# A macaron transformer layer on one core: first four rotary chunks in buffers of their own, rows sent by part, shorter plan distances at both ends, last value products ahead of the projection

## The chip, the cores and the metric

The kernel runs on one core of a Trainium2 chip. The metric is the device time of one execution in microseconds (us), lower is better. Times of the same kernel agree within about 0.3%.

## What is computed

The input x is 16 x 1024 x 256 in float32 (batch, positions, channels). The layer is a "macaron": half a feed-forward, attention, half a feed-forward, each with a layer norm in front and added to x.

```
x = x + 0.5 * ffn(layernorm(x))
x = x + attention(layernorm(x))
x = x + 0.5 * ffn(layernorm(x))

ffn(x):        prev = x shifted by one position
               xr, xk = mu_r*x + (1-mu_r)*prev,  mu_k*x + (1-mu_k)*prev
               sigmoid(xr @ W_r.T) * (relu(xk @ W_k.T)**2 @ W_v.T)
attention(x):  16 heads of size 16; q, k, v = x @ W_qkv + b_qkv
               rotary embedding on q and k; causal softmax(q k^T / 4) v
               y @ W_proj + b_proj
```

## The kernel before, in words

**Tiles.** A batch (1024 positions) is worked in 4 chunks of 256 positions (NCH). Attention takes heads in groups of 4 (G), so a batch has 4 groups and the kernel has 64, numbered n. A group's scores are worked in 12 ticks (a 512-wide query chunk by a 128-wide key block), 4 slots to a tick (one for each head): 48 slots a group (GSLOTS), 192 a batch (BSLOTS), 3072 in all. In one slot TensorE makes a score product (L585), ScalarE its exponential (L703) and, on diagonal blocks, GpSimd a causal select per tick (L922). Each tick then has value products (`pv`, L612). A softmax needs the row maximum first: 48 "units" per group, a product on TensorE (L592) and a masked maximum on VectorE (L806), run 61 slots ahead of the scores (MAX_FROM = -61). The units of one group follow those of the last without a break, so group 0 has its maxima in slots -61 to -14, group 1 from -13, group 2 from 35.

**Exact q and k in bf16.** The score products are bf16 with q and k split in three parts (high, mid, low), stacked as six 16-row terms on the partitions of `qr_sb` and `kr_sb`; a term names the part of q and of k (TERMS_Q, TERMS_K). To make them, each of the 2 x 4 rotary chunks of a batch (pair 0 or 1 of the head groups, chunk c; numbered i) runs through a chain over five engines: `r_QK` (L675, TensorE), `r_b0`, `r_b1` add the bias into `qb_sb` (L753, ScalarE), `r_swap` exchanges partitions by 4 DMAs into `sw_sb` (L525), `r_cos` (L963, GpSimd) and `r_sin` (L859, VectorE) multiply, `r_add` (L863) adds, `r_hi` (L762, ScalarE), `r_rest` (L966, GpSimd), `r_mid` (L765), `r_low` (L969) split into `part_sb`. `qb_sb` has two buffers and `sw_sb` one, so a chunk's bias waits for `r_low` of the chunk two before it, and a swap waits for `r_add` of the one before. When all 4 chunks of a pair are split, 12 DMAs of 128 KB for each group (steps `rows0` to `rows5`, one for k and one for q each, L534) carry them to `qr_sb` and `kr_sb`; the row `rows` of group n isn't planned before slot 48n - 95.

**Everything else is fitted in.** Feed-forward chunks p (`f_st`, `f_rstd`, `f_x`, `f_T`, `f_xn`, `f_dif`, `f_k`, `f_r`, then the matmul steps `f_K` L663, `f_R` L666, `f_V` L669 with `f_relu`, `f_sq`, `f_tanh`, then `f_u`, `f_xadd`), the layer norm of attention (`a_st`, `a_rstd`, `a_x`, `a_T`, `a_xn`), v (`a_V` L679, `a_vc`), the maximum's rows (`m_fin`, `m_T`, `m_copy`, `m_rows`), the output of attention (`y_copy` L787, `y_out`, `y_recip`, `y_back`, `y_in` through DRAM, `y_mul` L974), the projection (`p_P` L653 and L657, `xp` L871) and the stores are placed by `Plan`. Each step has an engine, a cost in slots' work, a start and a list of (step, number, distance): it may be placed once those steps lie at least that many slots back. The lowest start among the ready ones goes first; a matmul step also needs a free bank of two (`ps_d`). Outside slots -61 to 3071 an engine gets 2.5 times its normal work per slot. Slots are not times: each engine executes its instructions in the order of slots and waits for semaphores only. So the plan sets the order on each engine, and an empty slot costs nothing. The plan begins at slot FIRST; FIRST also sets the starts of the first batch's steps.

**Around the ends.** In the plan before, TensorE's order at the start is f_T.0, f_T.1, f_T.2, f_K.0, f_R.0, f_V.0, f_K.1, ...; the rotary chunks 0 to 3 come after one another; a_V.0 and a_V.1, then f_T.4, lie ahead of the first maximum unit and f_K.4, f_R.4, f_V.4 and r_QK.4 behind it. r_QK.7 ends in slot -1, r_low.7 is in slot 21 and the `rows` of group 2 in slots 23 to 28. At the end, p_P.60 and p_P.61 (first half of the last batch's projection) lie in slots 3073 to 3075, then the value products of the last two ticks (slot 3075), then f_T.124, f_T.125, f_K, f_R, f_V of 124 and 125, p_P.62, p_P.63, and the same for 126 and 127.

Of the kernel before, what the change touches and what calls it, by code (L numbers as in the profile page):

```python
# [18 lines left out]
CH = 256  # L19
# [10 lines left out]
NT = len(TERMS_Q)  # L30
KR = NT * HS
# [21 lines left out]
FIRST = -176  # L53


class Plan:
# [41 lines left out]
    def describe(self):  # L98
# [29 lines left out]
        for b in range(nb):  # L128
# [80 lines left out]
    def ready(self, slot, after):  # L209
        return all(k in self.slots and self.slots[k] + lag <= slot for k, lag in (((n, i), lag) for n, i, lag in after))  # L210
# [104 lines left out]
def macaron(nc, x, w_r, w_k, w_v, mu_r, mu_k, w_qk, b_qk, w_vv, b_v, w_p, b_p, rope_c, rope_s, out, nb=B):  # L315
# [6 lines left out]
    with ctx:  # L322
# [78 lines left out]
        swapped, r_cos, r_sin, r_add = sem("swapped"), sem("r_cos"), sem("r_sin"), sem("r_add")  # L401
# [81 lines left out]
        def _(eng):  # L483
# [28 lines left out]
            for slot in slots:  # L512
                for name, i in plan.at["SP"].get(slot, ()):
# [7 lines left out]
                    elif name == "r_swap":  # L521
                        sp.wait_ge(*taken_from("r_QK", i))
                        sp.wait_ge(r_add, i)
                        for q in range(4):
                            eng.dma_start(sw_sb[32 * q:32 * q + 32, :, :],  # L525
                                          qb_sb[32 * (q ^ 1):32 * (q ^ 1) + 32, i % 2, :, :]).then_inc(swapped, 16)
                    elif name[:4] == "rows":
                        b, g = divmod(i, NG)
                        ring, m, base = i % RS, g // 2, 64 * (g % 2)
                        sp.wait_ge(r_low, (2 * b + m + 1) * NCH)  # L530
                        sp.wait_ge(scored, GSLOTS * (i - RS + 1))
                        t = int(name[4:])
                        for dst, n, part in ((kr_sb, 1, TERMS_K[t]), (qr_sb, 0, TERMS_Q[t])):
# [38 lines left out]
        def _(eng):  # L572
# [110 lines left out]
            for slot in slots:  # L683
                if 0 <= slot < n_ticks * G:
# [353 lines left out]
```

## Time and profile before

| what | value |
|---|---|
| median of 3 executions | 3216.09 us (3215.34 to 3225.63) |
| profiled execution, whole | 3219.0 us |
| its span on the core | 3217.3 us |
| mean granted clock of TensorE | 0.979 |
| busy: TensorE / its weight loads | 95% / 52% |
| busy: VectorE, ScalarE, GpSimd | 77%, 68%, 46% |
| mean DMA rate | 76 GB/s |

The page cuts the span in 40 slices of 80.4 us, each digit a busy share in tenths. TensorE:

```profile
PE   5689999999999999999999999999999999999987
DVE  3678788887877878888887887888788888878852
PEclk8799999999999999999999999999999999999987
```

The reader sees 9 in all but the first three slices and the last two, and the granted clock lower only at both ends.

### The profile page before, as it was taken

What the parts mean: (1) busy time and instruction counts of PE and PEld (TensorE: products, weight loads), DVE (VectorE), ACT (ScalarE), POOL (GpSimd) and SP (SyncE); (2) the same over time, 40 slices, a digit from 0 to 9 for tenths busy, and PEclk for the clock granted to TensorE, in tenths of its full rate; (3) what the DMA queues carried; (4) which work ended last, traced back from release to release, by engine and by line L of the source; (5) the groups of instructions that cost most, each with busy time, mean ns of one, the idle gap of its engine ahead of it and who ended that gap; (6) DMA issues with size and microseconds to landing.
All of it is one profiled execution on the core that took longest, in us unless ns stands there. A gap on an engine that the chain in (4) does not pass through costs nothing.

```text
span 3217.3 us, 57438 instructions
## 1 busy us (share of the span) xinstructions
PE 3042.8 (95%) x18372; PEld 1664.5 (52%) x18372; DVE 2485.2 (77%) x8322; ACT 2182.1 (68%) x4801; POOL 1489.3 (46%) x2132
## 2 busy tenths in 40 slices
PE   5689999999999999999999999999999999999987
PEld 4434555555555555555555555555555555555434
DVE  3678788887877878888887887888788888878852
ACT  3266677777767777777776777777776777777663
POOL 4443444544544544444554444454454445444322
PEclk8799999999999999999999999999999999999987
DMA  3344244434434334433433434442443443344311
GB/s 90 50 67 79 61 84 86 76 79 74 93 59 96 77 73 88 76 87 67 96 68 75 91 72 84 80 82 69 81 97 60 85 88 75 80 74 84 74 41 34
DMA packets 201438, 245.30 MB, mean 76 GB/s; under 512 B 68269, under 2 KB 102321, under 8 KB 201137
## 3 DMA queue, kind: packets, MB, share of 16 engines
q1 hardware_dynamic: 201137, 241.63, 37.8%
q8 instruction: 147, 2.41, 0.4%
q14 instruction: 154, 1.26, 0.2%
HBM read 53.22 MB, written 51.38 MB: 33 GB/s over the span
## 4 chain that ended last, share of the span: by engine, by line
PE 81%; ACT 6%; DVE 6%; issue 3%; DMA 1%; POOL 1%; SPq 1%; POOLq 0%; DVEq 0%; ACTq 0%
PE ps_y L612 16%; PE ps_s L585 15%; PE ps_m L592 13%; PE ps_d L669 7%; PE ps_d L666 7%; PE ps_d L663 7%; PE ps_d L675 6%; PE ps_d L653 4%; ACT pt_sb L703 3%; DVE ps_m L806 3%; PE ps_d L679 3%; PE ps_d L619 3%; ACT qb_sb L753 1%; ACT xt_sb L712 1%; DVE fst_sb L819 1%
## 5 line engine op out<-in xcount | busy, mean ns | idle before, releaser
L806 DVE CUSTOM_DVE_ANT_0 ps_m<-ps_m,mask_sb 128x512 f32<-128x512 f32 (+3 forms) x3072 | 1692.4, 569 | 567.1 <-PE ps_m L592 550.8
L703 ACT ACTIVATE pt_sb<-ps_s 128x512 f32<-128x512 f32 (+3 forms) x3072 | 1470.5, 493 | 874.9 <-PE ps_s L585 852.7
L585 PE MATMUL ps_s<-qr_sb,kr_sb 99*128 99x512 bf16 (+3 forms) x3072 | 1009.4, 332 | 40.7 <-ACT pt_sb L703 30.9
L592 PE MATMUL ps_m<-kr_sb,qr_sb 96*128 96x512 bf16 (+3 forms) x3072 | 998.5, 328 | 33.6 <-DVE mx_sb L806 17.3
L922 POOL TENSOR_SCALAR_AFFINE_SELECT pt_sb<-pt_sb 128x512 f32<-128x512 f32 x512 | 334.4, 653 | 834.7 <-ACT pt_sb L703 831.7
L585 PEld LDWEIGHTS ps_s<-qr_sb,kr_sb 99*128 99x128 bf16 x3072 | 298.4, 98 | 783.6 <-ACT pt_sb L703 328.8
L612 PE MATMUL ps_y<-pt_sb,v_sb 128*32 128x512 f32 (+3 forms) x6144 | 636.8, 502 | 0.0
L806 DVE DVE_READ_ACCUMULATOR2_ANT mx_sb<- 128x1 f32 x3072 | 434.1, 141 | 0.0
L592 PEld LDWEIGHTS ps_m<-kr_sb,qr_sb 96*128 96x128 bf16 x3072 | 297.6, 97 | 168.1 <-DVE mx_sb L806 56.5
L675 PE MATMUL ps_d<-axn_sb,wqk_sb 128*128 128x256 f32 x1024 | 304.4, 396 | 3.9 <-ACT axn_sb L745 1.7
L663 PE MATMUL ps_d<-ka_sb,wk_sb 128*128 128x256 f32 x1024 | 301.9, 392 | 6.3 <-DVE ka_sb L830 4.6
L669 PE MATMUL ps_d<-wv_sb,ka_sb 128*128 128x256 f32 x1024 | 305.6, 387 | 0.0
L666 PE MATMUL ps_d<-wr_sb,dif_sb 128*128 128x256 f32 x1024 | 303.1, 384 | 1.8 <-ACT fxn_sb L727 1.8
L612 PEld LDWEIGHTS ps_y<-pt_sb,v_sb 128*32 128x32 f32 x6144 | 134.9, 109 | 259.1 <-issue 235.5
L950 POOL TENSOR_TENSOR x_sb<-x_sb,dif_sb 128x512 f32<-128x512 f32 x128 | 163.6, 1278 | 204.7 <-DVE dif_sb L842 202.9
L963 POOL TENSOR_TENSOR qb_sb<-qb_sb,cos_sb 128x512 f32<-128x512 f32 x128 | 178.0, 1390 | 118.8 <-DMA sw_sb<-qb_sb 117.4
L663 PEld LDWEIGHTS ps_d<-ka_sb,wk_sb 128*128 128x128 f32 x1024 | 194.5, 197 | 44.6 <-issue 6.4
L969 POOL TENSOR_TENSOR part_sb<-qb_sb,part_sb 128x512 bf16<-128x512 f32 x128 | 149.2, 1166 | 118.8 <-ACT part_sb L765 118.8
L675 PEld LDWEIGHTS ps_d<-axn_sb,wqk_sb 128*128 128x128 f32 x1024 | 184.1, 195 | 37.2 <-ACT fxn_sb L727 5.1
L666 PEld LDWEIGHTS ps_d<-wr_sb,dif_sb 128*128 128x128 f32 x1024 | 183.7, 193 | 31.9 <-ACT fxn_sb L727 2.6
L669 PEld LDWEIGHTS ps_d<-wv_sb,ka_sb 128*128 128x128 f32 x1024 | 180.3, 191 | 34.3
L619 PE MATMUL ps_d<-id_sb,xt_sb 128*128 128x128 f32 x768 | 125.2, 287 | 68.0 <-ACT xt_sb L712 48.7
(76 smaller groups left out, 3214.7 us busy)
## 6 DMA issues: line engine op xcount, KB each, us to landing
kr_sb<-part_sb SPq DMA_DIRECT2D x384, 128.0 KB, 4.5
qr_sb<-part_sb SPq DMA_DIRECT2D x384, 128.0 KB, 4.9
sw_sb<-qb_sb SPq DMA_DIRECT2D x512, 64.0 KB, 2.0
y_way<-yt_sb SPq DMA_DIRECT2D x128, 256.0 KB, 3.0
x_sb<-x SPq DMA_DIRECT2D x64, 256.0 KB, 2.9
yn_sb<-y_way SPq DMA_DIRECT2D x64, 256.0 KB
den_sb<-r_way SPq DMA_DIRECT2D x64, 256.0 KB
out<-x_sb SPq DMA_DIRECT2D x64, 256.0 KB, 2.2
```

The costliest lines, as they stand in the source:

```text
L585: eng.matmul(ps_s[:, slot % NS, 0:width], kr_sb[0:KR + NP, n % RS, j, kb * P:(kb + 1) * P], qr_sb[0:KR + NP, n % RS, j, q0:q0 + width], st ...
L592: eng.matmul(ps_m[:, u % NM, 0:width], qr_sb[0:KR, n % RS, j, i * P:(i + 1) * P], kr_sb[0:KR, n % RS, j, piece * QC:piece * QC + width], s ...
L612: pv_j = eng.matmul(ps_y[32 * j:32 * j + 32, QC - width:QC], v_sb[:, b % 2, kb, col:col + 32], pt_sb[:, tick % PT, j, 0:width], start=(kb ...
L619: last = eng.transpose(dst[:, cc * CH + t * P:cc * CH + (t + 1) * P], src[:, t, cc * P:(cc + 1) * P], id_sb[:, :])
L663: mm = eng.matmul(ps[:, rows], wk_sb[:, cc, cols], ka_sb[:, i % 2, cc, :], start=(cc == 0), stop=(cc == CC - 1))
L666: mm = eng.matmul(ps[:, rows], dif_sb[:, i % 2, cc, cols], wr_sb[:, cc, :], start=(cc == 0), stop=(cc == CC - 1))
L669: mm = eng.matmul(ps[:, rows], ka_sb[:, i % 2, cc, cols], wv_sb[:, cc, :], start=(cc == 0), stop=(cc == CC - 1))
L675: mm = eng.matmul(ps[:, rows], wqk_sb[:, cc, w0:w0 + P], axn_sb[:, c, cc, :], start=(cc == 0), stop=(cc == CC - 1))
L703: eng.activation(pt_sb[:, tick % PT, j, 0:width], ps_s[:, slot % NS, 0:width], ACT.Exp, scale=SCALE).then_inc(exped, 1)
L806: eng.tensor_tensor_reduce(ps_m[:, u % NM, 0:width], ps_m[:, u % NM, 0:width], mask_sb[:, m0:m0 + width], 1.0, -3e38, ALU.add, ALU.max, mx ...
L922: eng.affine_select(out=diag, in_=diag, compare_op=ALU.is_ge, fill=0.0, base=0, pattern=[[0, G], [1, P]], channel_multiplier=-1).then_inc( ...
L963: eng.tensor_tensor(qb_sb[:, i % 2, :, :], qb_sb[:, i % 2, :, :], cos, ALU.mult).then_inc(r_cos, 1)
```

## The change

It does seven things. (1) Rotary chunks 0 to 3 of the first batch keep their biased and swapped halves in `pt_sb` (the exponentials' buffer, not yet in use), each chunk in a place of its own, and don't wait for `r_low` or `r_add` of earlier chunks; chunks 4 and 5 don't wait for `r_low` either. (2) The semaphore `swapped` becomes four, one for each chunk number. (3) The six `rows` steps are sorted by part: steps 0 to 2 wait for the high parts only, 3 and 4 for the mid ones, 5 for the low ones. (4) FIRST goes from -176 to -160. (5) Distances count half (rounded up) before slot -61 and 0.4 (rounded up) from slot 3072 on. (6) Pair 1 of the first batch starts 10 slots earlier; for the last group, some distances on the way of y are shorter. (7) The value products of the last two ticks come at slot 3072, ahead of other steps, not at 3075.

```diff
-FIRST = -176
+BY_PART_Q = sorted(range(NT), key=lambda t: TERMS_Q[t])
+BY_PART_K = sorted(range(NT), key=lambda t: TERMS_K[t])
+FIRST = -160
...
-                        t = -40 + 18 * c if pair else FIRST + 32 + 6 * c
+                        t = -50 + 18 * c if pair else FIRST + 32 + 6 * c
...
-                    s("ACT", "r_b0", i, 0.36, t, ("r_QK", i, 1), ("r_low", i - 2, 1))
+                    s("ACT", "r_b0", i, 0.36, t, ("r_QK", i, 1), ("r_low", i - 2 if i >= NCH + 2 else -1, 1))
...
-                    s("SP", "r_swap", i, 3.2, t, ("r_b1", i, 1), ("r_add", i - 1, 1))
+                    s("SP", "r_swap", i, 3.2, t, ("r_b1", i, 1), ("r_add", i - 1 if i > NCH else -1, 1))
...
-                s("SP", f"rows{t}", n, 1.6, max(FIRST, at - 2 * GSLOTS + 1 + 3 * t), ("r_low", last, 2),
+                part = ("r_hi", "r_mid", "r_low")[TERMS_Q[BY_PART_Q[t]]]
+                s("SP", f"rows{t}", n, 1.6, max(FIRST, at - 2 * GSLOTS + 1 + 3 * t), (part, last, 2),
...
-                done = at + G * sum(KQ * (q + 1) for q in range(qc + 1)) + PV_AT
+                end = n == nb * NG - 1
+                done = at + G * sum(KQ * (q + 1) for q in range(qc + 1)) + (0 if end and qc == NQC - 1 else PV_AT)
...
-                s("DVE", "y_recip", k, 0.2, done + 1, ("y_out", k, 8))
+                s("DVE", "y_recip", k, 0.2, done + 1, ("y_out", k, 4 if end else 8))
...
-                    s("SP", "y_in", m, 1.6, done + 1, ("y_back", k, 6), ("y_mul", m - 1, 1), ("p_P", before, 1))
-                    s("POOL", "y_mul", m, 1.3, done + 1, ("y_in", m, 9))
+                    s("SP", "y_in", m, 1.6, done + 1, ("y_back", k, 3 if end else 6), ("y_mul", m - 1, 1), ("p_P", before, 1))
+                    s("POOL", "y_mul", m, 1.3, done + 1, ("y_in", m, 5 if end else 9))
...
+    def apart(self, slot, lag):
+
+        if slot >= self.nb * BSLOTS:
+            return math.ceil(lag * 0.4)
+        return math.ceil(lag * 0.5) if slot < MAX_FROM else lag
...
+        def swapped_of(i):
+
+            return pt_sb[:, 0, i, :].rearrange("p (k n) -> p k n", n=CH) if i < NCH else sw_sb[:, :, :]
+
+        def biased_of(i):
+
+            return pt_sb[:, 1, i, :].rearrange("p (k n) -> p k n", n=CH) if i < NCH else qb_sb[:, i % 2, :, :]
...
-                        sp.wait_ge(r_low, (2 * b + m + 1) * NCH)
+                        part, chunks = TERMS_Q[BY_PART_Q[k]], (2 * b + m + 1) * NCH
+                        if part == 0:
+                            sp.wait_ge(r_high, chunks)
+                        elif part == 1:
+                            sp.wait_ge(r_mid, chunks)
+                        else:
+                            sp.wait_ge(r_low, chunks)
...
             for slot in slots:
+                if slot == n_ticks * G:
+                    pv((n_ticks - 2, n_ticks - 1))
...
-                    act.wait_ge(r_low, i - 1)
+                    if i >= NCH + 2:
+                        act.wait_ge(r_low, i - 1)
```

## Rows read from the trace of the kernel before

**Rows 1.** The page's first part: busy time, share of the span, instructions.
```profile
PE 3042.8 (95%) x18372; PEld 1664.5 (52%) x18372; DVE 2485.2 (77%) x8322; ACT 2182.1 (68%) x4801; POOL 1489.3 (46%) x2132
```

**Rows 2.** Waits of TensorE, whole span: total us, times, longest.
```profile
PE ps_m L592 <- DMA qr_sb<-part_sb: 14.1, 2, 8.8
```

**Rows 3.** Chain that ended last, 0 to 201 us: start, us, piece.
```profile
29.57 1.73 PE ps_d L666 x8
...
53.81 2.03 DMA sw_sb<-qb_sb
...
85.29 1.16 POOL part_sb L969
86.47 0.62 SPq L534
...
93.54 9.08 DMA qr_sb<-part_sb
102.66 1.03 PE ps_m L592 x2
...
183.39 1.58 POOL part_sb L969
...
192.08 8.84 DMA qr_sb<-part_sb
```

**Rows 4.** Timeline, first feed-forward: start, us, engine, line, [idle before <- releaser].
```profile
15.37 0.88 DVE L830 SCALAR_TENSOR_TENSOR ka_sb<-dif_sb,muk_sb,fxn_sb 128x256 f32<-128x256 f32 x2 [2.51 <-POOL dif_sb L945]
...
18.67 3.62 PE L663 MATMUL ps_d<-ka_sb,wk_sb 128*128 128x256 f32 x8
...
49.01 1.89 PE L675 MATMUL ps_d<-axn_sb,wqk_sb 128*128 128x256 f32 x8
```

**Rows 5.** Timeline, rotary chunks 0 to 3 and what follows them.
```profile
51.00 0.84 ACT L753 ACTIVATE qb_sb<-ps_d,bqk_sb 128x256 f32<-128x256 f32 x2 [1.94 <-PE ps_d L675]
...
55.90 1.77 POOL L963 TENSOR_TENSOR qb_sb<-qb_sb,cos_sb 128x512 f32<-128x512 f32 x1 [2.91 <-DMA sw_sb<-qb_sb]
...
73.28 1.62 DVE L863 TENSOR_TENSOR qb_sb<-qb_sb,sw_sb 128x512 f32<-128x512 f32 x1 [1.15 <-POOL qb_sb L963]
...
83.39 1.15 POOL L966 TENSOR_TENSOR qb_sb<-qb_sb,part_sb 128x512 f32<-128x512 f32 x1 [1.29 <-ACT part_sb L762]
84.58 0.63 ACT L765 ACTIVATE part_sb<-qb_sb 128x512 bf16<-128x512 f32 x1 [1.26 <-POOL qb_sb L966]
...
92.41 0.88 DVE L830 SCALAR_TENSOR_TENSOR ka_sb<-dif_sb,muk_sb,fxn_sb 128x256 f32<-128x256 f32 x2 [8.81 <-POOL dif_sb L945]
```

**Rows 6.** Chain that ended last, from 3175 us: a feed-forward's matmul steps after idle.
```profile
3175.68 3.78 PE ps_d L663 x8
3179.47 2.22 PE ps_d L666 x8
3181.69 1.73 PE ps_d L669 x8
```

**Rows 7.** Stretches: length, busy us (instructions) PE, PEld, DVE, ACT, POOL, clock, DMA, GB/s.
```profile
100.00:110.00 10.00, 7.34 (x21) 5.22 (x22) 3.84 (x11) 1.23 (x2) 0.00 (x0) 0.58 0.29 30
...
130.00:140.00 10.00, 5.62 (x23) 3.05 (x22) 9.40 (x33) 2.43 (x5) 6.50 (x9) 0.78 0.30 44
...
150.00:160.00 10.00, 4.96 (x22) 2.43 (x21) 9.20 (x31) 1.74 (x5) 6.53 (x12) 0.81 0.01 3
...
200.00:210.00 10.00, 8.78 (x38) 2.73 (x38) 7.22 (x20) 4.06 (x11) 1.90 (x2) 0.66 0.14 30
210.00:220.00 10.00, 8.69 (x54) 4.33 (x52) 7.97 (x25) 5.69 (x14) 6.96 (x7) 0.83 0.41 69
```

**Rows 8.** Timeline of TensorE: first score, and the second wait for rows.
```profile
162.92 0.40 PE L585 MATMUL ps_s<-qr_sb,kr_sb 99*128 99x512 bf16 x1
...
200.96 0.61 PE L592 MATMUL ps_m<-kr_sb,qr_sb 96*128 96x512 bf16 x1 [5.28 <-DMA qr_sb<-part_sb]
```

**Rows 9.** Timeline, the last 60 us.
```profile
3162.58 2.05 PE L653 MATMUL ps_d<-wp_sb,yn_sb 128*128 128x256 f32 x4
...
3162.95 0.64 POOL L922 TENSOR_SCALAR_AFFINE_SELECT pt_sb<-pt_sb 128x512 f32<-128x512 f32 x1 [0.52 <-ACT pt_sb L703]
...
3168.66 0.86 PE L612 MATMUL ps_y<-pt_sb,v_sb 128*32 128x256 f32 x16
...
3199.46 3.78 PE L663 MATMUL ps_d<-ka_sb,wk_sb 128*128 128x256 f32 x8 [0.69 <-ACT fxn_sb L727]
```

**Rows 10.** Stretches as in rows 7, at the end.
```profile
3150.00:3160.00 10.00, 9.21 (x32) 1.43 (x28) 0.00 (x0) 4.74 (x11) 1.27 (x2) 0.50 0.00 0
3160.00:3170.00 10.00, 9.25 (x49) 5.40 (x48) 2.88 (x8) 1.80 (x7) 3.69 (x6) 0.67 0.00 0
```

More of the change, by code:

```diff
@@ L1 @@
+import math
 from contextlib import ExitStack
@@ L209, in ready @@
     def ready(self, slot, after):
-        return all(k in self.slots and self.slots[k] + lag <= slot for k, lag in (((n, i), lag) for n, i, lag in after))
+        return all((n, i) in self.slots and self.slots[n, i] + self.apart(slot, lag) <= slot for n, i, lag in after)
+    def apart(self, slot, lag):
+        if slot >= self.nb * BSLOTS:
+            return math.ceil(lag * 0.4)
+        return math.ceil(lag * 0.5) if slot < MAX_FROM else lag
     def place(self):
@@ L400, in macaron @@
         a_stat, a_mean, a_eps, a_pow, a_rstd, a_xt = sem("a_stat"), sem("a_mean"), sem("a_eps"), sem("a_pow"), sem("a_rstd"), sem("a_xt")
-        swapped, r_cos, r_sin, r_add = sem("swapped"), sem("r_cos"), sem("r_sin"), sem("r_add")
+        r_cos, r_sin, r_add = sem("r_cos"), sem("r_sin"), sem("r_add")
+        swapped = [sem(f"swapped{k}") for k in range(NCH)]
         r_high, r_rest, r_mid, r_low = sem("r_high"), sem("r_rest"), sem("r_mid"), sem("r_low")
@@ L522, in _ @@
                         sp.wait_ge(*taken_from("r_QK", i))
-                        sp.wait_ge(r_add, i)
+                        if i >= NCH:
+                            sp.wait_ge(r_add, i)
                         for q in range(4):
-                            eng.dma_start(sw_sb[32 * q:32 * q + 32, :, :],
-                                          qb_sb[32 * (q ^ 1):32 * (q ^ 1) + 32, i % 2, :, :]).then_inc(swapped, 16)
+                            eng.dma_start(swapped_of(i)[32 * q:32 * q + 32, :, :],
+                                          biased_of(i)[32 * (q ^ 1):32 * (q ^ 1) + 32, :, :]).then_inc(swapped[i % NCH], 16)
                     elif name[:4] == "rows":
                         b, g = divmod(i, NG)
-                        ring, m, base = i % RS, g // 2, 64 * (g % 2)
-                        sp.wait_ge(r_low, (2 * b + m + 1) * NCH)
+                        ring, m, base, k = i % RS, g // 2, 64 * (g % 2), int(name[4:])
+                        part, chunks = TERMS_Q[BY_PART_Q[k]], (2 * b + m + 1) * NCH
[5 more added lines that the diff above has]
+                            sp.wait_ge(r_low, chunks)
                         sp.wait_ge(scored, GSLOTS * (i - RS + 1))
-                        t = int(name[4:])
-                        for dst, n, part in ((kr_sb, 1, TERMS_K[t]), (qr_sb, 0, TERMS_Q[t])):
+                        for dst, n, t in ((kr_sb, 1, BY_PART_K[k]), (qr_sb, 0, BY_PART_Q[k])):
                             eng.dma_start(dst[t * HS:(t + 1) * HS, ring, :, :],
@@ L690, in _ @@
                 tick = slot // G - 1
-                if slot % G == PV_AT and 0 <= tick < n_ticks and tick % NTK not in BURST_OF:
+                if slot % G == PV_AT and 0 <= tick < n_ticks - 1 and tick % NTK not in BURST_OF:
                     pv((tick - 1, tick) if tick % NTK - 1 in BURST_OF else (tick,))
@@ L862, in dense @@
                     dve.wait_ge(r_sin, i + 1)
-                    eng.tensor_tensor(qb_sb[:, i % 2, :, :], qb_sb[:, i % 2, :, :], sw_sb[:, :, :], ALU.add).then_inc(r_add, 1)
+                    eng.tensor_tensor(biased_of(i), biased_of(i), swapped_of(i), ALU.add).then_inc(r_add, 1)
                 elif name == "b_add":
@@ L961, in dense @@
                     cos = cos_sb[:, halves(i % NCH)].rearrange("p (o n) -> p o n", o=1).broadcast_to([P, 2, CH])
-                    pool.wait_ge(swapped, 64 * (i + 1))
-                    eng.tensor_tensor(qb_sb[:, i % 2, :, :], qb_sb[:, i % 2, :, :], cos, ALU.mult).then_inc(r_cos, 1)
+                    pool.wait_ge(swapped[i % NCH], 64 * (i // NCH + 1))
+                    eng.tensor_tensor(biased_of(i), biased_of(i), cos, ALU.mult).then_inc(r_cos, 1)
                 elif name == "r_rest":
                     pool.wait_ge(r_high, i + 1)
-                    eng.tensor_tensor(qb_sb[:, i % 2, :, :], qb_sb[:, i % 2, :, :], parts_of(i, 0), ALU.subtract).then_inc(r_rest, 1)
+                    eng.tensor_tensor(biased_of(i), biased_of(i), parts_of(i, 0), ALU.subtract).then_inc(r_rest, 1)
                 elif name == "r_low":
                     pool.wait_ge(r_mid, i + 1)
-                    eng.tensor_tensor(parts_of(i, 2), qb_sb[:, i % 2, :, :], parts_of(i, 1), ALU.subtract).then_inc(r_low, 1)
+                    eng.tensor_tensor(parts_of(i, 2), biased_of(i), parts_of(i, 1), ALU.subtract).then_inc(r_low, 1)
                 elif name == "y_mul":
```

10 lines of the change are left out of this document (5 added, 5 removed).

## The prediction, made before the result was known

> **What bounds the kernel now.** I read the page first: TensorE is busy 95% of the span [rows 1], and the strip of forty slices has its gaps at both ends only. So the middle, some 3000 us, is one row of slots in TensorE's own order, and the change leaves its order nearly alone. A gain can only be the time until that row runs at its pace, and the time after it. The waits of TensorE say how much is to be had: two waits for the rows' DMAs make 14.1 us [rows 2]. The chain through the start says why: it goes from the swap DMAs to the last `r_low`, through 12 DMA issues by SP, through 9.08 us in which the last of them lands, to the first maximum at 102.66 [rows 3]. The same pattern stands once more before 200.96 [rows 3, 8]. Between them, VectorE is the fuller engine [rows 7]. The last views are those of the end [rows 6, 9, 10]: feed-forwards with a wait in front of each pair.
>
> **How I get the new order.** The plan is arithmetic with fixed costs, so I replayed its first and last hundred slots with the new distances, and then set durations from rows to the new order on each engine. That gives five terms.
>
> **Term 1, the start up to the first maximum.** *Feed-forward.* Before, f_K.0 starts at 18.67 behind f_T.2, though its input (15.37 + 0.88) is there at 16.25 [rows 4]. In the new order f_K.0 lies ahead of f_T.2 and starts at about 16.3. The halved distances also take f_V.1 behind f_T.3, a_T.0 behind f_K.2, and the first r_QK behind f_V.3 and a_T.2, where each input has been ready. Stepped on with 1.73 a matmul step [rows 3] and 0.6 for each bank that waits for ScalarE, r_QK.0 starts near 43.5 instead of 49.01 [rows 4]: 5.5 us. *Rotary.* SP issues a swap's four DMAs in 2.5 us, and the last lands 2.03 after its issue [rows 3]. With places of their own the four swaps follow one another from 46.4 on and land at 50.4, 52.9, 55.4 and 57.9. From there GpSimd is the limit. Its order is cos 0, 1, 2, rest 0, 1, cos 3, low 0, rest 2, low 1, low 2, rest 3, low 3; four times 1.77 and eight times 1.15 [rows 5] with two waits of 0.8 for swaps and one of 0.7 for r_mid give 50.5 + 18.6 = 69.1 for the end of r_low.3, before 86.45 (85.29 + 1.16) [rows 3]. r_hi.3 ends near 65.2. *Rows.* By part, the DMAs start at 65.2, not behind r_low; r_mid.3 and r_low.3 end before SP has issued the DMAs that need them. From the first issue at 86.47 to the first maximum it took 16.2 us [rows 3], and I keep all of it, since the transfers, not the issues, set it: landed at 81.4. *What is late next.* Not the rows. The new plan has f_K.4, f_R.4, f_V.4 and three quarters of r_QK.4 ahead of the first maximum, where before they lay behind it, and a_V.0 and a_V.1 now lie behind. f_K.4's input ended 93.29, 6.85 behind r_low.3 (92.41 + 0.88) [rows 5], because GpSimd's order has r_low.3 ahead of f_rstd.4. So it comes at 76.0, the step at 76.1; then 3.78 + 2.22 + 1.73 [rows 6] and 1.3 of r_QK.4 put the first maximum at 85.2. Before 102.66: **17.4 us**. The bounds: 21.3 were TensorE free when the rows land, 12 if GpSimd's waits fall 5 us worse.
>
> **A rule against this term.** VectorE's add took 1.62 us where GpSimd worked on its r_low [rows 5], though it moves no more than a swap's product with the sine; so packing both engines costs something, and I put VectorE's adds behind GpSimd's work and kept 1.77 for each cos. The Trainium skill (SBUF — State Buffer, Who interferes with whom) says that a VectorE instruction with two SBUF inputs and a GpSimd one that reads SBUF exclude each other for the whole instruction. Here the row agrees (1.62 is GpSimd's 1.15 and then some). Taken both ways, with GpSimd losing 0.5 on each of eight more instructions, the first maximum would come 4 us later.
>
> **Term 2, first maximum to first score.** 102.66 to 162.92 is 60.3 us [rows 3, 8] for 61 slots. VectorE is at 9.4 and 9.2 of 10 in two of the stretches but at 3.84 in the first, where TensorE ran f_K.4 between the maxima at a clock of 0.58 [rows 7]. With that work in front, the first maxima run at VectorE's pace. I take 5 us for this and 0.8 for f_u.4, also in front now. Against it, the m_rows of group 0 stand behind swap 7 in SP's queue (before, ahead of it): its four issues of 0.6 and a shorter distance to slot 0 cost about 1. Net **4.8 us**, between 0 and 8.
>
> **Term 3, the second wait.** r_QK.7 ends ten slots earlier, in slot -10 instead of -1, r_hi.7 comes in slot 4 and r_low.7 in slot 11, not 21, and the rows of group 2 start in slot 6 instead of 23. From r_low.7's end (184.97) to the landing it took 16 us [rows 3, 8]. Slot 35, where the first maximum of group 2 stands, was reached at 195.7. The new rows are there some 10 us ahead of it. The wait of 5.28 goes [rows 8]: **5.3 us**, certain if term 1 is right.
>
> **Term 4, after it.** After that wait the clock is 0.66 and 0.83 for 10 us each [rows 7], so 8.8 and 8.7 busy us hold at most 3.0 and 1.5 us that full clock would save, and SP, which was late with the 12 issues, is late with the rest (swaps 9 and 10, and the m_rows of group 1). I take **3 us**, between 0 and 6. The Trainium skill (TensorE: Matmul & The Clock Gate, What's actually happening) says that the throttled clock is the default and that activity releases it; the trace agrees, 0.66 stands behind the wait and 1.00 where none is.
>
> **The middle: 0.** Sorting the rows by part and four semaphores for one add no instruction. `rows` of later groups start at 48n - 95, where high and low are long done for one pair of groups; for the other, SP's rows step can come some slots earlier and wait. What is queued behind it on SP is swaps, y steps and stores, all with tens of slots in hand. No wait of TensorE for rows shows in the middle [rows 2].
>
> **Term 5, the end.** With the shorter way of y, y_mul.62 comes in slot 3059, not 3070, and p_P.60 and p_P.61 move into the last score ticks, slots 3062 to 3068. That is no gain by itself: the 8 steps are the same and run on TensorE, which is busy 9.21 of 10 us there [rows 10]. At half clock they cost as much as where they stood (four records in 2.05 [rows 9]). But the statistics of chunks 124 and 125, 3162 to 3171 before, now lie beside the ticks. The last value products then wait for GpSimd's last select (0.64, 3162.95 [rows 9]), about 1 us without cover, and end near 3170.5, 1 us later than before (3168.66 + 0.86). f_T.124 follows at once, f_K.124 at 3174.3 and not 3175.68 [rows 6]: 1.4. p_P.62 still comes behind f_V.125, by its start of 3084 against 3048, so the second wait stays, but in the new plan f_K.126 has the other bank and needn't wait the 0.69 for f_xn.127 [rows 9]: 0.6. **2 us**, between -2 and 6.
>
> **The sum.** 17.4 + 4.8 + 5.3 + 3 + 2 = 32.5 us. The profiled execution took 3219.0 (span 3217.3), which gives 3186.5 for one like it; the median of the three runs is 3216.1, 2.9 below, so I predict **3183.6**. The bounds of the terms, half used on each side, give 3172 to 3194 as this case's own range.
>
> **The rivals.**
> *Less than half reaches the end (3194 to 3204, chance 0.16).* The shorter distances put an instruction that isn't ready ahead of ones that are, in the order of GpSimd or TensorE. For it: cos 2 already stands ahead of rest 0 in my replay. Worked out: term 1 falls to 12 with the late GpSimd, term 2 to 0, term 4 to 0; with 5.3 and 0 at the end, 17 us are left, 3199.
> *The end gets its clock back (3170 to 3176, 0.14).* In the last ticks the clock is 0.50, and the projection's matmuls are where it rises (0.67) [rows 10]. If they release it inside the ticks, some 14 us of TensorE's work lie behind them up to the last value products, and up to half is saved; with 4 more of term 1, 3173. The Trainium skill (TensorE: Matmul & The Clock Gate, What's actually happening) would have it so, since activity releases the clock there.
> *It doesn't do what it says (within 0.3%, 3206 to 3226, 0.04).* The bias of chunk 2 goes without its wait, but if GpSimd's order kept chunks serial, the gain would be the 3.1 us from r_hi to r_low (83.39 to 86.45 [rows 3, 5]) twice.
> *Slower (0.04).* SP waits in order. If the rows steps that wait for high parts hold back a swap or y step by those 3.1 us for each of the 31 later pairs of groups, and that passes to TensorE, 96 us come against 32: 3280. It decides once SP's slack, tens of slots, is used up; from 1.05 us lost for each pair on, the gain of 32.5 is gone. Nothing in the waits of TensorE shows SP near that.
> The forecast's own range holds the other 0.62. The range for 8 in 10 takes in most of the clock rival and half of the first: 3171 to 3199. About 0.3% (10 us) is what a measurement of this kernel tells from no change: faster by more 0.91, within it 0.05, slower 0.04.
>
> **What would show it.** The first maximum (L592) at 85, with f_V.4 (L669) just ahead of it and no wait for `qr_sb<-part_sb` of over 1 us; the last `r_low` of chunk 3 at 69; the first score at 140; no wait near slot 35, at about 173; the last score near 3138, then one value-product group, with L653 records between the scores before it. Wrong would be a first maximum after 91 (term 1), a wait for the rows' DMAs in the second place (term 3), or a distance from the first score of group 3 to that of group 63 changed by over 3 us (the middle).

## The result and the profile after

The changed kernel takes **3179.44 us** (median of 4 runs, 3177.07 to 3184.35) against 3215.72 for the one before beside it (4 runs, 3210.74 to 3225.63): ratio 0.9885, 95% interval 0.9859 to 0.9912. The medians lie 36.3 us apart, and the interval makes that 28 to 45. Its profiled execution took 3180.46 us with a span of 3178.7, where that of before had 3219.0 and 3217.3.

The page of the changed kernel, against [rows 1] and the strips shown with the time before: TensorE has 16.7 us less of busy time for the same 18372 matmuls, so these matmuls ran at a higher clock on average; the other 21.9 of the 38.6 us between the spans are idle time gone.

```profile
PE 3026.1 (95%) x18372; PEld 1656.0 (52%) x18372; DVE 2484.0 (78%) x8322; ACT 2183.1 (69%) x4801; POOL 1489.9 (47%) x2132
...
PE   4899999999999999999999999999999999999988
...
PEclk8999999999999999999999999999999999999997
```

The waits of TensorE after the change (total us, times, longest). None for `qr_sb<-part_sb` of [rows 2] is left; the longest is now f_T.4's.

```profile
PE ps_d L645 <- ACT xt_sb L740: 54.7, 34, 19.9
...
PE ps_m L618 <- DVE mx_sb L835: 11.5, 40, 1.1
```

Its timeline through the rotary chunks (start, us, engine, line, idle before and releaser): r_QK.0 to r_QK.2 in one row, cos 0, rest 0 and rest 1 in one row, the add of chunk 2, the sine of chunk 3, the rows' first issue, r_low.3, f_T.4, f_K.4, f_V.4, the first maximum, the first score, the first maximum of group 2 (slot 35), and `y_copy.2`, where the row of slots runs at its pace.

```profile
43.73 5.45 PE L701 MATMUL ps_d<-axn_sb,wqk_sb 128*128 128x256 f32 x24 [0.62 <-DVE dif_sb L871]
...
50.69 1.77 POOL L992 TENSOR_TENSOR pt_sb<-pt_sb,cos_sb 128x512 f32<-128x512 f32 x1 [2.90 <-DMA pt_sb<-pt_sb]
...
57.48 2.71 POOL L995 TENSOR_TENSOR pt_sb<-pt_sb,part_sb 128x512 f32<-128x512 f32 x2
57.55 1.62 DVE L892 TENSOR_TENSOR pt_sb<-pt_sb 128x512 f32<-128x512 f32 x1 [1.15 <-POOL pt_sb L992]
59.10 1.64 DVE L888 TENSOR_TENSOR pt_sb<-pt_sb,sin_sb 128x512 f32<-128x512 f32 x1
...
65.73 0.61 SPq L560 DMA_DIRECT2D kr_sb<-part_sb  x1
...
68.60 1.15 POOL L998 TENSOR_TENSOR part_sb<-pt_sb,part_sb 128x512 bf16<-128x512 f32 x1 [0.74 <-ACT part_sb L794]
...
72.69 1.09 PE L645 MATMUL ps_d<-id_sb,xt_sb 128*128 128x128 f32 x4 [19.87 <-ACT xt_sb L740]
76.76 3.48 PE L689 MATMUL ps_d<-ka_sb,wk_sb 128*128 128x256 f32 x8 [2.98 <-DVE ka_sb L859]
81.80 1.89 PE L695 MATMUL ps_d<-wv_sb,ka_sb 128*128 128x256 f32 x8
84.82 0.38 PE L618 MATMUL ps_m<-kr_sb,qr_sb 96*128 96x512 bf16 x1
...
142.17 0.38 PE L611 MATMUL ps_s<-qr_sb,kr_sb 99*128 99x512 bf16 x1
...
174.75 0.38 PE L618 MATMUL ps_m<-kr_sb,qr_sb 96*128 96x512 bf16 x1
...
200.44 0.59 ACT L816 ACTIVATE yt_sb<-ps_y 128x512 f32<-128x512 f32 x1
```

The end, from the last ticks on: a projection step among the scores, the last value products, f_K.124.

```profile
3124.30 1.14 PE L679 MATMUL ps_d<-wp_sb,yn_sb 128*128 128x256 f32 x4
...
3133.02 0.86 PE L638 MATMUL ps_y<-pt_sb,v_sb 128*32 128x256 f32 x16 [1.18 <-POOL pt_sb L951]
...
3137.51 3.75 PE L689 MATMUL ps_d<-ka_sb,wk_sb 128*128 128x256 f32 x8 [0.21 <-DVE ka_sb L859]
```

Four **marks** cut the span into the prediction's terms: the first maximum, the first score, `y_copy.2` (the third copy of value products, behind the second wait), and `y_copy.60`, 1368 us later in both. From the single pair of traces, and from the means over four kernels that have the start of before (before, before_again, fill_before, end_alone) and four that have the changed start (after, u_end, fill_end, fill_u_end):

| stretch | predicted | pair of traces | means |
|---|---|---|---|
| r_QK.0 (part of the next) | 5.5 | 49.01 - 43.73 = 5.3 | 48.0 - 43.9 = 4.1 |
| term 1, to the first maximum | 17.4 | 102.66 - 84.82 = 17.8 | 101.7 - 85.6 = 16.0 |
| term 2, on to the first score | 4.8 | 20.8 - 17.8 = 2.9 | 18.5 - 16.0 = 2.4 |
| terms 3 and 4, on to y_copy.2 | 8.3 | 32.05 - 20.75 = 11.3 | 30.6 - 18.5 = 12.1 |
| middle, on to y_copy.60 | 0 | 0.1 | -0.8 |
| term 5, the end | 2 | 38.6 - 32.1 = 6.5 | 3.2 (timed, end_alone) |
| sum | 32.5 | 38.6 | 33.0 |

One trace's marks vary by chance: `y_copy.2` lies at 231.1 to 232.5 in the four of the old start and at 200.4 to 202.3 in those of the new one, and the end (span less `y_copy.60`) takes 1604.7 to 1610.6 in six kernels with the changed end (1608.5 in the mean). In the experiments below the start of a kernel is therefore set against the means. The -0.8 of the middle comes from fill_u_end, which lost 2.3 us there with no edit in that stretch.

### The profile page after: what moved, and what is told of

It is laid out like the page before. It is cut to its first block, busy times and chain, and to the rows that moved or that the text cites. A ratio compares the mean times of both kernels' runs of the same rounds, so it can differ in the third digit from the quotient of the medians.

```text
span 3178.7 us, 57430 instructions
## 1 busy us (share of the span) xinstructions
PE 3026.1 (95%) x18372; PEld 1656.0 (52%) x18372; DVE 2484.0 (78%) x8322; ACT 2183.1 (69%) x4801; POOL 1489.9 (47%) x2132
## 4 chain that ended last, share of the span: by engine, by line
PE 82%; DVE 6%; ACT 6%; issue 3%; POOL 1%; DMA 1%; SPq 0%; POOLq 0%; DVEq 0%; ACTq 0%
PE ps_y L638 17%; PE ps_s L611 16%; PE ps_m L618 13%; PE ps_d L695 7%; PE ps_d L692 7%; PE ps_d L689 7%; PE ps_d L701 6%; PE ps_d L679 4%; DVE ps_m L835 3%; ACT pt_sb L731 3%; PE ps_d L705 3%; PE ps_d L645 3%; ACT qb_sb L782 1%; ACT xt_sb L740 1%; DVE fst_sb L848 1%
## 5 line engine op out<-in xcount | busy, mean ns | idle before, releaser
L689 PEld LDWEIGHTS ps_d<-ka_sb,wk_sb 128*128 128x128 f32 x1024 | 194.5, 197 | 47.0 <-issue 10.9
```

The source lines that it names most:

```text
L689: mm = eng.matmul(ps[:, rows], wk_sb[:, cc, cols], ka_sb[:, i % 2, cc, :], start=(cc == 0), stop=(cc == CC - 1))
```

## The experiments

Where an expectation speaks of Theory A and B, A is the account that I held when it was written, B its rival. No kernel leaves out a part of the computation. Those that add products write them to a bank that nobody reads. Marks are from one profiled execution each, times with an interval from several.

**u_places: chunks 0 to 3 back in the shared buffers.**

```diff
-            return pt_sb[:, 0, i, :].rearrange("p (k n) -> p k n", n=CH) if i < NCH else sw_sb[:, :, :]
+            return sw_sb[:, :, :]
...
-            return pt_sb[:, 1, i, :].rearrange("p (k n) -> p k n", n=CH) if i < NCH else qb_sb[:, i % 2, :, :]
+            return qb_sb[:, i % 2, :, :]
...
-                        if i >= NCH:
-                            sp.wait_ge(r_add, i)
+                        sp.wait_ge(r_add, i)
```

> The changed kernel with one part undone: rotary chunks 0 to 3 share qb_sb and sw_sb again, with their waits; all distances and orders else stay. Theory A (the shared buffers held the rotary stage, and GpSimd takes over as its limit once they are gone): the last r_low of chunk 3 ends near 81 instead of 69.8, the first maximum comes near 97 instead of 84.8, and the steady shift against the kernel before falls from 32.1 to about 20 us; whole time near 3192. Theory B (the gain at the start comes from the new order on TensorE alone, the buffers are hidden behind it): first maximum stays within 3 us of 84.8, whole time within 4 us of 3180.

The timeline of u_places (first maximum, `y_copy.2`), and below it one of its waits of TensorE (total, times, longest), which the changed kernel does not have: r_QK behind a bias that waits for its buffer.

```profile
94.98 0.38 PE L617 MATMUL ps_m<-kr_sb,qr_sb 96*128 96x512 bf16 x1
...
210.41 0.59 ACT L814 ACTIVATE yt_sb<-ps_y 128x512 f32<-128x512 f32 x1
```

```profile
PE ps_d L700 <- ACT qb_sb L780: 9.3, 1, 9.3
```

First maximum 9.4 later than 85.6, `y_copy.2` 9.1 later than 201.3. The shared buffers held the rotary stage, as A had it, though A put the loss at 12, and what is lost there is lost to the end of the start. It is the largest single part.

**u_part: all six rows steps behind r_low.**

```diff
-                part = ("r_hi", "r_mid", "r_low")[TERMS_Q[BY_PART_Q[t]]]
+                part = "r_low"
...
-                        if part == 0:
...
+                        sp.wait_ge(r_low, chunks)
```

> The changed kernel with the rows steps all waiting for the low parts again, terms in the sorted order. Theory A (in the first group TensorE waits for the feed-forward chunk 4, not for the rows, so a few us later rows cost little): rows DMAs start 4.0 us later (69.8, not 65.7), land near 86, first maximum 1 to 2 us later, the middle's shift falls by 1 to 3 us. Theory B (rows set the first maximum in the changed kernel): the full 4 us at the first maximum, and 4 more at the second group of rows; shift falls by 6 to 8 us.

The timeline of u_part: first maximum, first maximum of group 2, `y_copy.2`.

```profile
86.89 0.38 PE L613 MATMUL ps_m<-kr_sb,qr_sb 96*128 96x512 bf16 x1
...
179.63 0.61 PE L613 MATMUL ps_m<-kr_sb,qr_sb 96*128 96x512 bf16 x1 [2.67 <-DMA qr_sb<-part_sb]
...
206.98 0.59 ACT L811 ACTIVATE yt_sb<-ps_y 128x512 f32<-128x512 f32 x1
```

From r_QK.0 (45.03 here) the first maximum comes after 41.9 us, against 41.7 in the changed kernels. So sending by part brings nothing there: with the rows' DMAs begun only after r_low, TensorE still does not wait for them, since it is busy with ffn 4 and r_QK.4 up to the maximum. It is close, as the last of these DMAs landed at 86.4 by the trace. For the second pair it brings more than A had it and less than B: a wait of 2.67 us returns, and `y_copy.2` is 5.7 later, of which 1.1 was lost ahead of r_QK.0 already, by chance.

**u_dist: full distances and FIRST = -176 at the start.**

```diff
-FIRST = -160
+FIRST = -176
...
-        return math.ceil(lag * 0.5) if slot < MAX_FROM else lag
+        return lag
```

> The changed kernel with full distances before slot -61 and the start back at -176, so the order on TensorE at the start is f_T.0, f_T.1, f_T.2, f_K.0 again, and f_K.4, f_R.4, f_V.4 lie behind the first maximum. Theory A (order alone gave 5 us of the rotary stage's start, and having feed-forward 4 in front gave some 5 us more behind the first maximum): first r_QK at 49, first maximum at 87 to 90, steady shift 8 us smaller (24). Theory B (distances only change empty slots, which cost nothing): shift stays 32 within 1 us.

The timeline of u_dist, first maximum and `y_copy.2`.

```profile
90.27 0.60 PE L618 MATMUL ps_m<-kr_sb,qr_sb 96*128 96x512 bf16 x2 [2.19 <-DMA qr_sb<-part_sb]
...
205.64 0.59 ACT L816 ACTIVATE yt_sb<-ps_y 128x512 f32<-128x512 f32 x1
```

r_QK.0 starts at 46.0, and not at 49 as A expected. That doesn't split the head's 4.1 us: up to r_QK.0 the plan of u_dist has the order of before on TensorE, and the four kernels with the start of before begin r_QK.0 anywhere from 46.4 to 49.0 (end_alone 46.42). One execution can't tell how much of the 4.1 the distances are. The first maximum now waits for rows, since ffn 4 has gone behind it. `y_copy.2` is 4.3 later, half of what A had.

**u_pair: pair 1 back to its old start.**

```diff
-                        t = -50 + 18 * c if pair else FIRST + 32 + 6 * c
+                        t = -40 + 18 * c if pair else FIRST + 32 + 6 * c
```

> The changed kernel with pair 1 of the first batch back at start -40, so r_QK.7 ends in slot -1 instead of -8. Theory A (the second wait went because these rows come earlier): TensorE waits 1 to 5 us for the rows' DMAs in slot 35 again, steady shift smaller by 2 to 6 us. Theory B (the second wait went because the start before it is shorter in the queue of SP, whatever the slots of pair 1): no wait for rows, shift within 1 us of 32.1.

The timeline of u_pair: first maximum, first score, a score that waits for the row of maxima (`m_rows`) of group 1, `y_copy.2`.

```profile
84.32 0.81 PE L618 MATMUL ps_m<-kr_sb,qr_sb 96*128 96x512 bf16 x3
...
140.02 0.38 PE L611 MATMUL ps_s<-qr_sb,kr_sb 99*128 99x512 bf16 x1
...
183.70 0.59 PE L611 MATMUL ps_s<-qr_sb,kr_sb 99*128 99x512 bf16 x1 [1.38 <-DMA qr_sb<-mt_sb]
...
201.86 0.59 ACT L816 ACTIVATE yt_sb<-ps_y 128x512 f32<-128x512 f32 x1
```

No wait for rows returns, and `y_copy.2` moves by 0.6, within chance. The first score comes 3.3 us earlier than the mean of 143.3 (1.3 of it ahead of the first maximum, where r_QK.4 no longer stands), and 3.8 are lost behind it. So the earlier start of pair 1 only moves work of r_QK and of the rotary steps from behind the first score to ahead of it. B's outcome came, and my reading that this start removes the second wait fell; B's reason, the shorter start in SP's queue, was not tried by itself.

**ffn4_late: ffn 4 behind the first maxima, as before.** This asks whether my "what is late next" was worth anything: the rows are there first, so TensorE could begin the maxima at once.

```diff
-            return -60 + 20 * c
+            return (-40 if c == 0 else -60) + 20 * c
```

> The changed kernel with feed-forward chunk 4 released 20 slots later, so f_K.4, f_R.4, f_V.4 lie behind the first maximum again (slots -37 to -32) and only r_QK.4 lies ahead. Theory A (feed-forward 4 sets the first maximum, 3 us behind the rows, but its matmul steps cost 5 us later if they don't run there): first maximum at 81.5 to 82.5, set by the rows' DMAs, steady shift within 2 us of 32.1, more likely smaller. Theory B (the stage behind is bound by VectorE alone, so TensorE's work there is free): shift 3 us larger.

The timeline of ffn4_late, first maximum and `y_copy.2`.

```profile
81.07 4.14 PE L618 MATMUL ps_m<-kr_sb,qr_sb 96*128 96x512 bf16 x7 [25.66 <-DMA qr_sb<-part_sb]
...
203.21 0.59 ACT L816 ACTIVATE yt_sb<-ps_y 128x512 f32<-128x512 f32 x1
```

The first maximum comes at 81.07, 4.5 us earlier and within 0.4 of the 81.4 that I worked out for the rows alone. But TensorE has waited 25.66 us with nothing to do, `y_copy.2` is 1.9 later and `y_copy.60` 3.5 later (1573.18 against a mean of 1569.66). The early mark is no gain: ffn 4 has to be done somewhere, and in that wait it is nearly free. How much its place is worth stays rough, since 1.6 of the 3.5 were lost behind `y_copy.2`, where fill_u_end lost 2.3 with no edit there.

**u_end: the way of y as long as before.** The distance of y_in to y_back goes back to 6 as well.

```diff
-                s("DVE", "y_recip", k, 0.2, done + 1, ("y_out", k, 4 if end else 8))
+                s("DVE", "y_recip", k, 0.2, done + 1, ("y_out", k, 8))
...
-                    s("POOL", "y_mul", m, 1.3, done + 1, ("y_in", m, 5 if end else 9))
+                    s("POOL", "y_mul", m, 1.3, done + 1, ("y_in", m, 9))
```

> The changed kernel with the distances on the way of y of the last group as before (8, 6, 9), so the projection p_P.60 and p_P.61 lies behind the last score, in slots 3072 to 3074, not among the last score ticks. Theory A (these matmuls among the ticks raise the granted clock in the last 8 us of the scores, and that is most of the 6.6 us gained at the end): the clock stays 0.50 up to the last score, and of the 6.6 us at the end 1 to 3 are left; whole time 4 to 5 us longer. Theory B (the statistics of chunks 124 and 125 beside the ticks are what gains): the clock moves little and 5 us are lost by a longer way from p_P.60 to f_K.124.

A stretch of u_end ahead of its projection (length, busy us of PE, PEld, DVE, ACT, POOL with instructions, granted clock, DMA share, GB/s):

```profile
3110.00:3120.00 10.00, 8.50 (x44) 1.40 (x36) 0.25 (x1) 6.67 (x13) 0.02 (x1) 0.88 0.24 80
```

The end took 1611.67 us from `y_copy.60`, with 1610.61 in the changed kernel. In this kernel too the clock rose inside the last ticks, at 0.88 in this stretch, though the projection stood behind them. So p_P among the scores is not needed to release it. The time by itself doesn't part the theories. But the low clock of the last ticks lasted 20 us here, as in u_part and u_places, whose ends took 1604.7 and 1605.8 with the shorter way of y. So at the clock as it comes the shorter way may be worth more than one profile against one shows; that is not settled. The next five runs bear on the clock and on the order.

**fill_end: one more product in each of the last 60 slots.** A bf16 product of 128 x 512 is added wherever the maximum units have run out.

```diff
+FILLED = 60
...
+            def fill(slot):
+                pe.wait_ge(max_taken, n_groups * NU)
+                eng.matmul(ps_m[:, slot % NM, :], idb_sb[:, :], mask_sb[:, 0:QC], start=True, stop=True)
...
+                elif n_ticks * G - FILLED <= slot < n_ticks * G:
+                    fill(slot)
```

> The changed kernel with one more product in each of the last 60 score slots, where the maxima have ended: identity (bf16, 128x128) by the mask (128x512), written to a free bank of ps_m that nobody reads. Theory A (in the last 45 us the granted clock is 0.50 because TensorE has too little to do per tick, and filling it brings the clock back): clock 1.00 over most of this stretch, a full tick takes 3.2 to 3.5 us instead of 4.19, and the end comes 5 to 9 us earlier. Theory B (the clock is low for another reason, such as the wait for the maximum's rows ahead of this stretch): the clock stays 0.50, each fill costs 0.43 us, and the end comes 15 to 25 us later.

Stretches of the changed kernel, in the same columns:

```profile
3100.00:3110.00 10.00, 8.64 (x41) 1.90 (x36) 0.25 (x1) 5.72 (x13) 0.96 (x2) 0.50 0.08 27
3110.00:3120.00 10.00, 9.24 (x30) 1.22 (x26) 0.00 (x0) 4.97 (x10) 0.00 (x0) 0.50 0.20 55
3120.00:3130.00 10.00, 9.71 (x51) 4.10 (x51) 1.69 (x5) 4.94 (x11) 2.81 (x4) 0.77 0.00 0
```

and the first two of them in fill_end:

```profile
3100.00:3110.00 10.00, 9.52 (x63) 2.69 (x64) 0.25 (x1) 7.30 (x17) 1.27 (x2) 1.00 0.09 30
3110.00:3120.00 10.00, 9.61 (x52) 2.70 (x52) 0.00 (x0) 6.66 (x13) 1.87 (x2) 1.00 0.15 52
```

With more matmuls in the same 10 us (63 against 41), the clock stays at 1.00, and the end takes 1604.19 instead of 1610.61 (1604.7 to 1610.6 in the six kernels with this end and no fills). All ten profiles without fills have a stretch of 20 to 44 us at the lower level in the last ticks, and none of the four with them has one there. So the last ticks are slow because the clock falls to its lower level there, and it falls once the maximum units have run out and TensorE has less work per slot (A). A busy share of 8.64 or 9.24 hides this: the records are long because the clock is low.

**fill_before and fill_u_end: the same fills in the kernel before, and in u_end.** With the clock at 1.00 in all the last ticks, the order of the end can be judged with less of its luck. The edits are those above.

> The kernel before the change with the same fills as in fill_end (one product of the identity by the mask in each of the last 60 score slots). Compared with fill_end from output copy 60 to the end, it tells what the change of the end brings with the clock at 1.00 in both. fill_end took 1604.2 us from there, the kernel before 1617.1, the changed one 1610.6. Theory A (the change of the end brings 2 us in itself, as its steps add up, and the rest of the 6.5 came from a shorter stretch at half clock): fill_before takes 1606 to 1607.5. Theory B (the order in itself brings 4 us or more, because the projection fits beside the score ticks for nothing): fill_before takes 1608 or more.

> fill_end with the projection p_P.60 and p_P.61 behind the last score (the distances on the way of y as before: 8, 6, 9), other parts of the change's end kept. Theory A (the placement of the projection among the ticks is the larger part of what the end gains at equal clock): from output copy 60 to the end 1.5 to 4 us more than fill_end's 1604.2. Theory B (the shorter distances and the earlier last value products gain, the projection's place doesn't): within 0.7 us of 1604.2.

The end takes 1605.52 in fill_before, 1604.19 in fill_end and 1605.89 in fill_u_end. So the new order of the end is worth some 1.3 us where the clock is held, and the shorter way of y (1.7) would be all of it. Both agree with A. Each is the difference of two single executions, so a few tenths to a us of it can be chance.

**before_again: the kernel before, unchanged.** How much of the 6.5 us was that one profile?

> The kernel before, unchanged, looked at once more. In the runs so far the stretch at half clock in the last group of the changed kernel's order was 20.5 or 34.1 us long with the same code of the end. Theory A (its length differs from execution to execution): from output copy 60 to the end this look takes 1611 to 1616 us, not 1617.1, or about the same with a stretch of another length than 44.4. Theory B (the kernel before always has the long one): 1617 within 0.5 and 44 us again.

Stretches of before_again, which answer to [rows 10]:

```profile
3140.00:3150.00 10.00, 8.80 (x38) 1.47 (x36) 0.00 (x0) 6.50 (x12) 0.48 (x1) 0.76 0.17 54
3150.00:3160.00 10.00, 8.07 (x48) 4.23 (x46) 1.58 (x5) 3.95 (x12) 3.24 (x5) 1.00 0.00 0
```

Its end took 1609.66 us; in the profile of before it took 1617.09. The same code, the same middle, and 7.4 us between them (the 17 timed executions of this kernel beside end_alone spread over 11.9 us): here the clock rose in 3140 to 3150, in the other only after 3160, behind the projection [rows 10]. My pair of traces compared an unlucky end with a middling one.

**end_alone: parts 5 (end only), 6 (way of y) and 7 in the kernel before.**

```diff
+    def apart(self, slot, lag):
+        return math.ceil(lag * 0.4) if slot >= self.nb * BSLOTS else lag
...
+                if slot == n_ticks * G:
+                    pv((n_ticks - 2, n_ticks - 1))
```

> The kernel before with only the change of the end: distances by 0.4 from slot 3072 on, the shorter way of y of the last group, last value products at slot 3072. Theory A (order alone 1.3 us, as at full clock, and on top a shorter stretch at half clock in most executions, since the projection lies in it): median 3 to 7 us below the kernel before. Theory B (the 6.5 us of the one profile were mostly luck of that execution's clock): median within 3 us of the kernel before.

3209.91 us (12 runs, 3208.73 to 3213.83) against 3214.67 (17 runs, 3209.52 to 3221.41); the ratio is 0.9990, interval 0.9981 to 0.9998, which is 3.2 us, between 0.6 and 6.1 (the two medians lie 4.8 apart). That is inside or at the lower edge of A's 3 to 7, and B's "within 3" is not shut out by the interval. It is the one timed measure of term 5.

**warm_all: fills at the end and in four waits.** If the clock is the cost, it can be bought back elsewhere: around f_T.4, behind f_T.124, p_P.63 and f_T.126 TensorE waits, and the f_K that follows runs at half clock (3.48 and 3.75 us in the changed kernel, where 1.89 is a step's usual record).

```diff
+WARM = {("f_T", 4, 0): 6, ("f_T", 124, 0): 6, ("p_P", 63, 3): 12, ("f_T", 126, 0): 6}
...
+            def warm(count):
+                for k in range(count):
+                    eng.matmul(ps_m[:, k % NM, :], idb_sb[:, :], mask_sb[:, 0:QC], start=True, stop=True)
...
+                    if (name, i) == ("f_T", 4):
+                        pe.wait_ge(f_rstd, 5)
+                        warm(3)
...
+                    warm(WARM.get((name, i, u), 0))
```

> fill_end and, besides, the same filling products in four waits of TensorE ahead of feed-forward steps that run at half clock: 3 before and 6 behind f_T.4, 6 behind f_T.124, 12 behind p_P.63, 6 behind f_T.126. Theory A (an engine kept busy in a wait starts its next step at full clock): f_K.4 takes 1.73 to 2 us instead of 3.48, f_K.126 2 instead of 3.7; first maximum 1.5 us earlier against the first r_QK; whole time 9 to 11 us below the changed kernel's, near 3170, and 3 us below fill_end. Theory B (the fills delay the transposes behind them as much as they save): whole time within 1.5 us of fill_end's 3176.5.

The timeline of warm_all: fills ahead of f_K.4 and f_K.4 itself, fills behind p_P.63, f_K.126.

```profile
73.96 1.75 PE L624 MATMUL ps_m<-mask_sb,idb_sb 128*128 128x512 bf16 x6
...
77.15 1.97 PE L701 MATMUL ps_d<-ka_sb,wk_sb 128*128 128x256 f32 x8 [1.44 <-DVE ka_sb L877]
...
3143.60 2.75 PE L624 MATMUL ps_m<-mask_sb,idb_sb 128*128 128x512 bf16 x12
...
3150.29 1.96 PE L701 MATMUL ps_d<-ka_sb,wk_sb 128*128 128x256 f32 x8 [0.69 <-DVE ka_sb L877]
```

3168.57 us (median of 4 runs, 3167.22 to 3172.97) against 3212.54 for before; the ratio is 0.9865, interval 0.9849 to 0.9882. It is the fastest kernel here: 10.9 us under the changed one by their medians, but 7.7 if each is set against the kernel before that was timed beside it, and the intervals of the two ratios overlap. f_K.4 takes 1.97 instead of 3.48, f_K.126 1.96 instead of 3.75, the first maximum is at 83.70, and the end takes 1600.52, 3.7 less than fill_end.

## Why the prediction came out right, step by step

**The whole.** 3183.6 was forecast and 3179.4 measured, inside the range. The sum of 32.5 stands against 33.0 by the means and 36.3 by the medians of time. The total is better than its terms: 2 is too large, 3 with 4 too small, and only 1 and the middle are right in size and reason. Terms 2 to 4 together are 13.1 against 14.2 and 14.5, since their errors are one: work that I left behind the first score lies ahead of it.

**Term 1: right in mechanism and size** (17.4; 17.8 in the pair, 16.0 in the means). The replay of the order held at each mark: r_QK.0 at 43.73 (43.5), the end of r_low.3 at 69.75 (69.1), the rows' first issue at 65.73 (65.2), f_K.4 at 76.76 (76.1), the first maximum at 84.82 (85.2) behind f_V.4 without a wait for rows. u_places shows that 9 us of it are the shared buffers, and ffn4_late that the rows would have landed at 81, as worked out. The head's 5.5 us is 4.1 by the means, and no run divides it. The one thing I gave to it wrongly is sending by part: u_part shows 0.2 us there.

**The rule against it.** Both engines paid, GpSimd less than the rule taken both ways would have it. The add took 1.62 where most later ones take 0.69. On GpSimd the four cos took 1.71 to 1.77 against 1.27 for most later ones, which I had in the sum; of the eight others, rest 1 and rest 2 took 1.60 and not 1.15 (rest 0 and 1 are the row of 2.71 above), and the r_low stayed near 1.15. That is 0.9 us for GpSimd, where 4 were the price. The Trainium skill (SBUF — State Buffer, Who interferes with whom) has one of such a pair wait for the other's whole instruction, and the trace agrees: the add that started at 57.55 ended at 59.17, 0.54 behind rest 0, and rest 1 ended 1.02 behind the add.

**Term 2: too large** (4.8; 2.9 and 2.4). What failed is that I costed the earlier pair 1 at nothing here. u_pair has the first score at 140.02, where I had put it, and it differs from the changed kernel in that start alone: the rotary work ahead of the first score costs 3.3 us, 2.0 of it behind the first maximum. Against the means of the old start, u_pair has 4.4 us for this term, where I had 4.8.

**Term 3: right that the wait goes, wrong in why.** No wait for rows is left. But I called it certain from term 1 and gave it to the earlier slots, of which the replay was off too: in the plan r_QK.7 ends in slot -8, not -10, r_low.7 lies in 16, not 11, and the rows of group 2 in 11 to 18, not from 6. u_pair keeps the wait away without the earlier start, and u_part brings 2.67 of the 5.28 back with it. Sending by part is what removes the last of it. The earlier start buys only margin: by the trace the last rows of group 2 landed at 168.6 and were wanted at 174.75, and in u_pair at 170.8 and 172.6. I had 10 us of margin and it is 6.

**Term 4: mis-sized** (terms 3 and 4: 8.3; 11.3 and 12.1). The 3.8 us too little are those that u_pair loses behind the first score: against the means of the old start it has 8.2 here, and the forecast's 8.3 is that of a kernel without the earlier pair. The waits and the clock show where they lie. I counted the clock from 200 to 220 only and took 3 of the 4.5 us there. Between the two levels, 1.2 and 2.4 GHz, a mean granted clock of c over 10 us costs 10 (1 - c): 3.4 and 1.7 for the 0.66 and 0.83 of [rows 7], and 1.5 more for a stretch of before that I had not read:

```profile
160.00:170.00 10.00, 9.84 (x46) 6.28 (x49) 7.22 (x22) 7.37 (x16) 3.94 (x5) 0.85 0.10 26
```

Nor had I counted a second wait of before in this stretch, for the `m_rows` of group 1 (timeline):

```profile
213.29 0.39 PE L585 MATMUL ps_s<-qr_sb,kr_sb 99*128 99x512 bf16 x1 [1.16 <-DMA qr_sb<-mt_sb]
```

In the changed kernel every stretch from the first score at 142.17 to `y_copy.2` is at 1.00, and it has no such wait:

```profile
140.00:150.00 10.00, 8.67 (x45) 4.87 (x47) 10.00 (x34) 6.61 (x14) 4.76 (x9) 1.00 0.11 26
...
160.00:170.00 10.00, 9.17 (x63) 3.86 (x62) 6.09 (x22) 8.09 (x17) 4.91 (x5) 1.00 0.97 136
170.00:180.00 10.00, 9.04 (x53) 2.73 (x51) 9.33 (x35) 8.73 (x18) 5.19 (x8) 1.00 0.12 29
```

5.28 and 1.16 of wait and 6.6 of clock, the clock times TensorE's busy share of about 0.9, are 12.4, against 11.3 of the pair and 12.1 of the means; it was argued from these rows and not tried by itself. In u_pair the wait for `m_rows` (1.38) and a stretch at 0.83 (180 to 190) are back. And a low clock does not need a wait ahead of it, as the forecast had it: 0.50 stands in [rows 10] beside 9.21 busy us.

**The middle: right.** Every `y_copy` from 3 to 120 is 31.8 to 32.1 us earlier than before. The slower rival had its place here and did not come.

**Term 5: its 2 us are nearer to the timed size than the trace's 6.5.** In time it is 3.2 (0.6 to 6.1); with the clock held it is 1.3 by single executions. The rest of the 6.5 is when the clock rises in the last ticks, which before_again moves by 7.4 us with no edit at all. So the 38.6 of the pair, against 36.3 in time, is in part luck of the two profiles. The last score came at 3131.61 and not near 3138; the half clock of the last ticks lasted 34 us here and 44 in before. The rival in which the end gets its clock back happened in part (0.77 in 3120 to 3130), but its mechanism is not needed: in u_end and before_again, with the projection behind the ticks, the clock rose there as well. f_K.124 comes 3.6 us behind the end of the last value products (3133.88 to 3137.51), where before it was 6.2 (3169.52 to 3175.68 [rows 6, 9]), so with the statistics beside the ticks this piece is 2.5 us shorter. I had 2.4 for it (3170.5 to 3174.3), less 1 for value products that wait uncovered, and they do wait (1.18 for GpSimd's select).

**What stays open.** The four undone parts cost 9.1, 5.7, 4.3 and 0.6 us at `y_copy.2`, 19.7 together, and the change brought 30.6. Presumably each part covers some of another's loss; no two were undone together. What the shorter way of y is worth at the clock as it comes is open too (1.7 with it held, 6 to 7 by u_end against u_part and u_places), and so is what ends the half clock in the last ticks sooner in one profile than in another.

## What to carry over

Replay the order of every engine and set durations from rows to it: that gave a start of 85 us within 1 us at each mark, and what is late next is then read off (here the work that fills a wait, not the transfer that ended it). Judge a gain at a mark behind the whole disturbed stretch, since u_pair and ffn4_late win 3.3 and 4.5 us at an early mark and have lost them by `y_copy.2`. And before a few us at one end are given to an edit, look at the same kernel's second profile: here it moved 7.4 us by itself.

## What the runs showed of the hardware

TensorE with 8.6 to 9.2 busy us in 10 by its records can sit at its lower clock for tens of microseconds (0.50, the 1.2 GHz level, from 3100 to 3120), and one 128 x 512 bf16 product more in each slot held it at 1.00. With its 60 products more, fill_end's end is 6.4 us shorter than that of the changed kernel's profile, and 4.3 shorter than the mean of the six kernels with that end. Products in a wait do the same for the step behind it: 1.97 for f_K.4 instead of 3.48. The Trainium skill (TensorE: Matmul & The Clock Gate, What's actually happening) has the throttled clock as the default and activity as what lifts it, and fill_end agrees. How long the lower clock lasts varied between two profiles of one program, 44 us in before and 24 in before_again, and their ends differ by 7.4 us.
